# A graph-attention layer in split fp32 on one core: the pairs' projections and values rewritten as pairs of 64-row matmuls

## The reference, cut to what matters

```
h  = relu(layernorm(x))                       # 384 x 1024
q, k, v    = h @ wq.T + bq, h @ wk.T + bk, h @ wv.T + bv
q2, k2, v2 = q @ wiq.T + biq, k @ wik.T + bik, v @ wiv.T + biv    # each (16 heads, 384, 64)
mask = -inf, softplus(w[type]) where an edge is (the last one wins), w[3] on the empty diagonal
attn = softmax(q2 @ k2.T / 8 + mask)          # per head, 384 x 384
y = x + (attn @ v2) @ wo.T + bo
```

## Time and profile before

| | us |
|---|---|
| median of 3 runs | 294.5 |
| span of the profiled execution | 292.6 |
| TensorE busy (1809 matmuls) | 286.9 |
| VectorE busy | 176.3 |
| ScalarE busy | 153.7 |
| GpSimd busy | 149.9 |

### The profile page before, as it was taken

The page is one execution under the profiler, slowest core; times in us unless marked ns, Lnnn a source line. Parts: engine busy times, 40 slices in busy tenths (PEclk is TensorE's granted clock), DMA queues, the critical chain, the costliest instruction groups (busy, mean ns, idle before and its releaser), DMA issues.

```text
span 292.6 us, 4992 instructions
## 1 busy us (share of the span) xinstructions
PE 286.9 (98%) x1809; PEld 266.0 (91%) x1809; DVE 176.3 (60%) x473; ACT 153.7 (53%) x289; POOL 149.9 (51%) x156
## 2 busy tenths in 40 slices
PE   6999999999999999999999999999999999999996
PEld 3799998888899999999999999999999997888885
DVE  4999878696534543454377676665748475835241
ACT  2986343242542344234434685969687879774100
POOL 6452454453454544644400796748393939873000
PEclk9999999999999999999999999999999999999999
DMA  7969965839643344324454043040403122400032
GB/s 269 324 237 266 330 219 165 249 113 341 222 143 106 112 144 146 116 100 146 164 212 146 0 147 119 26 147 0 146 23 124 50 97 72 146 0 0 2 143 72
DMA packets 15818, 40.84 MB, mean 140 GB/s; under 512 B 3481, under 2 KB 4914, under 8 KB 15794
## 3 DMA queue, kind: packets, MB, share of 16 engines
q1 hardware_dynamic: 13346, 38.53, 39.6%
q0 software_dynamic: 2016, 1.21, 1.5%
q10 hardware_dynamic: 432, 0.79, 0.7%
HBM read 37.71 MB, written 2.81 MB: 138 GB/s over the span
## 4 chain that ended last, share of the span: by engine, by line
PE 96%; DMA 1%; DVE 1%; ACT 0%; POOL 0%; issue 0%
PE banks L884 27%; PE banks L885 26%; PE banks L886 26%; PE banks L1015 5%; PE banks L1058 3%; PE banks L1059 3%; PE banks L1030 3%; PE banks L1043 1%; DMA x_sb<-in_x 1%; PE banks L935 1%; DVE stats L711 1%; PE banks L975 1%; PE banks L965 0%; PE banks L978 0%; ACT x_sb L504 0%; POOL rstd L384 0%
## 5 line engine op out<-in xcount | busy, mean ns | idle before, releaser
L426 POOL DMA_INDIRECT cells<-value,cell x51 | 54.5, 1069 | 60.2 <-DMA cells<-value,cell 47.5
L479 ACT ACTIVATE w_hi<-raw 128x1024 fp32r<-128x1024 f32 x50 | 52.6, 1053 | 19.5 <-PE banks L886 17.3
L886 PE MATMUL banks<-a_lo,w_hi 128*128 128x384 f32 x184 | 61.5, 334 | 0.0
L884 PE MATMUL banks<-a_hi,w_hi 128*128 128x384 f32 x184 | 61.5, 334 | 0.0
L885 PE MATMUL banks<-a_hi,w_lo 128*128 128x384 f32 x184 | 61.5, 334 | 0.0
L747 DVE TENSOR_TENSOR w_lo<-raw,w_hi 128x1024 fp32r<-128x1024 f32 x36 | 44.2, 1229 | 12.4 <-ACT w_hi L479 12.2
L452 POOL TENSOR_SCALAR prob<-prob,row_inv 128x384 f32<-128x384 f32 x36 | 22.6, 645 | 42.6 <-DVE row_inv L814 42.6
L884 PEld LDWEIGHTS banks<-a_hi,w_hi 128*128 128x128 f32 x184 | 34.5, 188 | 0.0
L885 PEld LDWEIGHTS banks<-a_hi,w_lo 128*128 128x128 f32 x184 | 34.5, 188 | 0.0
L886 PEld LDWEIGHTS banks<-a_lo,w_hi 128*128 128x128 f32 x184 | 34.5, 188 | 0.0
L399 POOL TENSOR_TENSOR w_lo<-raw,w_hi 128x1024 fp32r<-128x1024 f32 x14 | 33.7, 2410 | 0.0
(11 more groups left out here) (151 smaller groups left out, 611.0 us busy)
## 6 DMA issues: line engine op xcount, KB each, us to landing
raw<-in_slabs SPq DMA_DIRECT2D x56, 512.0 KB, 3.4
work<-key_rows SPq DMA_DIRECT2D x6, 256.0 KB, 5.6
prob<-key_rows SPq DMA_DIRECT2D x6, 256.0 KB, 3.9
x_sb<-in_x SPq DMA_DIRECT2D x3, 512.0 KB, 5.2
out_y<-x_sb SPq DMA_DIRECT2D x5, 256.0 KB, 2.1
cells<-prob SPq DMA_DIRECT2D x2, 576.0 KB, 7.6
cells<-value,cell POOLq DMA_INDIRECT x51, 3.7
x_sb<-in_x ACTq DMA_DIRECT2D x3, 256.0 KB, 4.4
```

The lines of the kernel that those rows point to most:

```text
L426: nc.gpsimd.indirect_dma_start(out=cells[c][:, :], out_offset=bass.IndirectOffsetOnAxis(ap=cell[:, t:t + 1], axis=0), in_=value[:, t:t + 1 ...
L479: nc.scalar.activation(split_place(s)[0], raw[:, s % RAW, :], ACT.Copy).then_inc(slab_hi, 1)
L884: nc.tensor.matmul(psum, w[0], a[0], start=first, stop=False)
L886: return nc.tensor.matmul(psum, w[0], a[1], start=False, stop=last)
```

## The change

It keeps the matrices, the split and the load of the slabs' bytes, and changes how the pairs are worked:

- The q and k projections come out of tiles that hold 64 rows of q above the same 64 rows of k: slabs 16 to 31 alternate between wq and wk and are written interleaved, in twos, into the ring. The second projections are 64-row matmuls, q2 on rows 0 to 63 beside k2 on rows 64 to 127, each into its own bank (`pair_steps`; 48 row pairs for a pair of heads). Slabs 32 to 47 hold one half of the rows of wiq above one of wik.
- `v2` is laid out by 64-row blocks, and so read out in 24 + 24 instructions of 64 x 256 in place of 6 + 6 of 128 x 512.
- The values of both heads run beside each other (`pair_values`, 12 row pairs), with 64 nodes a block; the turns of all eight pairs are 64 by 64, in three runs of 12 (`turn`), the second and the third one behind the other from step 1 on.
- The turned probabilities are read out in three instructions of 768 elements a pair on ACT and on DVE in place of six of 384; reciprocals go in threes.
- q2, k2 and the pair's projection banks (4 and 5) have one buffer; scores and turns share banks 0 to 3, the values have 6 and 7.
- `y_part` moves between the `max_part` of step 0. The output pieces have other banks and another order.
- Early scratch tiles share memory with `prob`, and the bias rows of q and k are copied once (`bias_parts`).

The diff, cut to its core:

```diff
-LO_ALL = QK0 + TILES_AHEAD + 3
+LO_ALL = QK0 + 2 + AHEAD
+SLABS_OF_STEP = [((37 + 2 * j,), (38 + 2 * j,)) for j in range(PAIRS - 1)] + [((51, 52), (53,)), ((54, 55), ())]
...
+        def pair_place(pair):
+            return 6 if pair == 1 else 4
...
+        def last_of(s):
+            return s + 1 - s % 2 if Q0 <= s < QK0 else s
+
         def wait_split_place(eng, s):
...
-                eng.wait_ge(slab_used, s - RING + 1)
+                eng.wait_ge(slab_used, last_of(s) - RING + 1)
...
+            def v2_hi_part(g):
+                for t in range(NT):
...
+                    for half in range(2):
+                        for x in range(2):
+                            own, _ = rows_of(x)
+                            nc.scalar.activation(v2[own, 2 * t + half, pairs_of(g), x, :], v2_from(g, t, half, x),
+                                                 ACT.Copy).then_inc(v2_hi, 1)
...
@@ block.scalar
             for j in range(PAIRS + 1):
+                first, second = SLABS_OF_STEP[j]
+                if 2 <= j < PAIRS:
+                    pair_hi_part(j - 2)
+                for s in first:
+                    split_hi(s)
                 if j < PAIRS:
+                    for n in range(NT):
+                        exp_part(j, n)
                 if j >= 1:
+                    for m in range(2):
+                        pt_hi_part(j - 1, m)
+                if j == PAIRS:
+                    pair_hi_part(PAIRS - 2)
+                if j >= 1:
+                    pt_hi_part(j - 1, 2)
+                if j < PAIRS - 1:
+                    for second_of in range(2):
+                        tile_hi_part(3 * KT + 2 * (j + 1) + second_of)
+                for s in second:
+                    split_hi(s)
+                if j >= 1:
+                    half_part(j - 1)
...
@@ block.vector
             for j in range(PAIRS + 1):
                 if j < PAIRS:
+                    max_part(j, 0)
+                    if j == 0:
+                        y_part(0)
+                    max_part(j, 1)
+                    inv_part(j, 0)
+                    if j == 0:
+                        y_part(1)
+                    max_part(j, 2)
+                    inv_part(j, 1)
+                    if j == 0:
+                        y_part(2)
+                    inv_part(j, 2)
                 if j >= 1:
+                    for m in range(2):
+                        pt_lo_part(j - 1, m)
                 if j == PAIRS:
                     pair_lo_part(PAIRS - 2)
+                if j >= 1:
+                    pt_lo_part(j - 1, 2)
+                if j < PAIRS - 1:
+                    for second_of in range(2):
+                        tile_lo_part(3 * KT + 2 * (j + 1) + second_of)
+                if j >= 1:
+                    head_part(j - 1)
...
+            def pair_steps(pair, first, end):
+                if first == 0:
+                    pe.wait_ge(v2_lo, 4 * GS * NT)
+                    if pair >= 1:
+                        pe.wait_ge(tile_lo, 3 * KT + (0, 0, 2, 6)[pair] if pair < 4 else 3 * KT + 2 * pair)
+                for step in range(first, end):
+                    half, k, p = step // STEPS, step % STEPS // 3, step % 3
...
+                    for x in range(2):
+                        own, _ = rows_of(x)
+                        mm = nc.tensor.matmul(bank[pair_place(pair) + x][:, 0:N], w[own, k * P:(k + 1) * P],
+                                              a[own, block_at % KT, :], start=(step == 0), stop=(step == 2 * STEPS - 1))
...
             def scores(j, n):
+                if n == 0:
+                    pe.wait_ge(tile_lo, 3 * KT + 2 * (j + 1))
+                if n == 2:
+                    pe.wait_ge(masked, chunk_at(j, 0, 1) + 1)
...
+            def turn(pair, m):
+                at, j = turn_place(m), pair + 1
...
+                if m == 2:
+                    pe.wait_ge(pt_lo_ok, turn_at(pair, 0) + 1)
...
+            def pair_values(pair):
...
+                order = [(b, p) for b in range(4) for p in range(2)] + [(b, p) for p in range(2) for b in (4, 5)]
+                for i, (b, p) in enumerate(order):
+                    pe.wait_ge((pt_hi_ok, pt_lo_ok)[p], turn_at(pair, b // 2) + 1)
...
+            pair_steps(0, 0, 2 * STEPS)
+            pair_steps(1, 0, FIRST_STEPS)
+            scores(0, 0)
+            pair_steps(1, FIRST_STEPS, 30)
+            scores(0, 1)
+            pair_steps(1, 30, 40)
+            scores(0, 2)
+            pair_steps(1, 40, 48)
+            pair_steps(2, 0, 8)
+            for j in range(1, PAIRS - 1):
+                scores(j, 0)
+                pair_steps(j + 1, 8, 16)
+                scores(j, 1)
+                pair_steps(j + 1, 16, 24)
+                scores(j, 2)
+                pair_steps(j + 1, 24, 32)
+                turn(j - 1, 0)
+                pair_steps(j + 1, 32, 44)
+                turn(j - 1, 1)
+                turn(j - 1, 2)
+                pair_steps(j + 1, 44, 48)
+                pair_values(j - 1)
+                if j < PAIRS - 2:
+                    pair_steps(j + 2, 0, 8)
+            last = PAIRS - 1
+            scores(last, 0)
+            scores(last, 1)
+            pe.wait_ge(tile_lo, 5 * KT)
+            out_part(0, range(0, 3))
+            scores(last, 2)
+            turn(last - 1, 0)
+            out_part(1, range(0, 3))
+            turn(last - 1, 1)
+            turn(last - 1, 2)
+            out_part(0, range(3, 5))
+            pair_values(last - 1)
+            turn(last, 0)
+            turn(last, 1)
+            out_part(1, range(3, 5))
+            for n in range(2):
+                out_part(n, range(5, 6))
+            turn(last, 2)
+            for n in range(2):
+                out_part(n, range(6, 7))
+            pair_values(last)
+            out_part(2, range(0, 7))
+            out_part(3, range(0, 7))
...
```

More of the change, by code:

```diff
@@ L217, in as_turned, with score_place @@
             return a[:, k, :] if k < KT - 1 else a[:, k, :].rearrange("p (t m) -> p t m", m=P)
[L219 to L236, removed]
+        def score_place(n):
+            return (0, 2, 0)[n]
@@ L627, in _, with pt_hi_part, half_part @@
-            half_part(H - 1)
+            def pt_hi_part(pair, m):
+                both = pair * ROW_BLOCKS + 2 * m + 2
+                act.wait_ge(pt_done, both)
+                act.wait_ge(pt_done_high, both)
+                if pair >= 1:
+                    act.wait_ge(head_done, pair)
+                nc.scalar.activation(as_turned_probs(pt_hi, m), turned(m), ACT.Copy).then_inc(pt_hi_ok, 1)
+            def half_part(pair):
+                act.wait_ge(head_done, pair + 1)
+                b = BIV + pair
+                for x in range(2):
+                    own, other = rows_of(x)
+                    nc.scalar.activation(half_sum[own, :], head_bank[x][other, 0:N], ACT.Identity,
+                                         bias=bias[own, b:b + 1]).then_inc(half_ok, 1)
@@ new lines, in pt_lo_part, with head_part @@
+            def pt_lo_part(pair, m):
+                dve.wait_ge(pt_hi_ok, turn_at(pair, m) + 1)
+                nc.vector.tensor_tensor(as_turned_probs(pt_lo, m), turned(m),
+                                        as_turned_probs(pt_hi, m).bitcast(F32), ALU.subtract).then_inc(pt_lo_ok, 1)
+            def head_part(pair):
+                for x in range(2):
+                    own, _ = rows_of(x)
+                    dve.wait_ge(half_ok, 2 * pair + x + 1)
+                    if x == 0 and pair >= 1:
+                        dve.wait_ge(head_lo, pair)
+                    nc.vector.tensor_tensor(head_out[own, :], head_bank[x][own, 0:N], half_sum[own, :],
+                                            ALU.add).then_inc(head_sum, 1)
@@ new lines, in pair_values @@
+            def pair_values(pair):
+                if pair >= 1:
+                    pe.wait_ge(head_sum, 2 * pair)
+                else:
+                    pe.wait_ge(tile_lo, 3 * KT + 4)
+                order = [(b, p) for b in range(4) for p in range(2)] + [(b, p) for p in range(2) for b in (4, 5)]
+                for i, (b, p) in enumerate(order):
+                    pe.wait_ge((pt_hi_ok, pt_lo_ok)[p], turn_at(pair, b // 2) + 1)
+                    for x in range(2):
+                        own, _ = rows_of(x)
+                        w = v2[own, b, pair, :, :].rearrange("p c d -> p (c d)")
+                        mm = nc.tensor.matmul(head_bank[x][:, 0:N], w, (pt_hi, pt_lo)[p][own, b, :],
+                                              start=(i == 0), stop=(i == len(order) - 1))
```

506 lines of the change are left out of this document (199 added, 307 removed).

## The result

The changed kernel takes 377.39 us (median of six runs, 374.31 to 378.20); the kernel before, run beside it, 294.44. The ratio is 1.279, with the 95% interval 1.274 to 1.284. The forecast was 299.7 us in a range of 294.0 to 303.5: slower, as forecast, but by 27.9% where 1.8% was forecast, and most of it by a cause that the forecast doesn't have. The profiled execution has a span of 372.6 us.

What follows compares the result with a forecast made beforehand. TensorE was taken as the bound. Own work -4.9, the step's chain +5.4, step 0 +1.1 and the end +3.8 us gave +5.4, taken as +5.2: from 294.5 to 299.7 us, range 294.0 to 303.5.

Steps and rivals of the forecast that it cites:

- What I cost at nothing: Items given no time: small `v2` reads, paired slabs, strided operands, POOL's order, SP's loads; lost `v2` cover up to 0.5 us.
- more waits than I see: Rival: further waits, as slabs split too late at the end or first q tiles held by `v2`; 303 to 308 us, chance 0.07.
- The first q tiles: Before the pairs: the second twelve small `v2` reads lie under the first two q and k tiles, enough by 0.1; no cost.
- TensorE's own work: Matmul work: 16 fewer switches between full and half rows, -3.2 us, and cheaper turns, -1.7 us; together -4.9 us.
- the rival of a lost pace: Rival: half rows lose pace in long stretches as weight loads come into the open; about 340 us, chance 0.03.
- The step's chain: Steps 1 to 6: next projections wait for `tile_lo` behind the `pt_lo` reads, 0.9 us six times; +5.4 us.
- the slope: Read-out times for 768 elements extended from 384 and 512: ACT 0.81 us, DVE 0.96 us.
- Step 0: Before pair 1's scores: `y_part` between `max_part` makes DVE's work 8.9 us against TensorE's 7.8; +1.1 us.
- The end: From step 7 on: TensorE waits behind splits, `pt_lo` and `head_lo`, 1.8, 1.2 and 0.8 us; +3.8 us.
- the signs of being wrong: Projections following values without a gap, wide reads under 0.6 us, or ACT's end splits not ahead of its `pt_hi`.
- The first rival: Wide reads cost less than the slope, hiding the step's chain; 293.2 us, or 290 to 291 with the end hidden; chance 0.14.

Runs made afterwards that it cites:

- e1: The changed kernel with slabs 32 to 47 laid out by the host so that each loads as one whole block; 305.74 us, ratio 1.040.
- e7: e1 with the second run of turns at matmul step 36 instead of 44 and the third at 42; 302.38 us, ratio 1.027.
- e9: e5 with pair 6's subtraction done by GpSimd between its splits instead of by VectorE; 293.36 us, ratio 0.9946.
- e10: e1 with the y additions moved from VectorE's step 0 to the query and key stage, and four more matmul steps in step 0; 305.76 us.
- e5: e1 with the edits of e7, e8 and e10, and the first query tile read out ahead of v2's second half; 296.63 us.
- e8: e1 with late splits behind read-outs and norms, pair 6's copy and subtraction behind pair 7's first read-out, its third turns behind the next output piece; 302.69 us.
- e4: e1 with the second run of turns moved from matmul step 44 to 36 and the third to 46; 307.01 us, ratio 1.045.

## Why the prediction was wrong, step by step

**The step that failed** is the last sentence of "What I cost at nothing": "SP issues the same loads; the half slabs have the same bytes." The number of loads and of bytes is the same, and each took some 10.1 us on two engines where whole slabs landed in 3.4 to 3.5 us before. It cost 71.7 of the 77.7 us between forecast and result. The sum costed a transfer by its bytes and never looked at its shape; nor did a rival, "more waits than I see" included. That the result is slower, as forecast, is to that extent luck.

The other 6.0 us are e1 (305.7) against the forecast; they too end above the range. The rival "more waits than I see" (303 to 308 us, 0.07) has this time and one of its causes, the first q tiles held by `v2`. By the terms of the sum, in e1's trace (its rows of the pairs' start and of the first scores stand first):

```profile
146.42 0.44 PE L1062 MATMUL banks<-b_hi,w_hi 64*128 64x384 f32 x2
146.70 0.34 PE L1062 MATMUL banks<-b_hi,w_lo 64*128 64x384 f32 x2
...
158.31 0.35 PE L1081 MATMUL banks<-k_hi,q_hi 64*128 64x384 f32 x2
```

- **The first q tiles: cost at nothing ("enough by 0.1"), +2.05 us** (the pairs start at 146.42 against 144.37). The small reads take 0.40 (ACT) and 0.45 us (VectorE) back to back, forecast 0.28 and 0.33: twelve are 4.8 and 5.4 us, not 3.4 and 4.0. VectorE came to tile 8 at 87.24, and TensorE waited for it until 88.01, with its last matmul started at 86.06.
- **TensorE's own work: -4.9, too large by about 2.** The pace of half rows held: the 67 places from 146.70 to 158.31 are 0.173 us each, weight loads included. So the rival of a lost pace did not come. By the rule of the Trainium skill beside it ("TensorE: Matmul & The Clock Gate", Part 3, The mechanism) each place would have paid for its load; the trace disagrees, now over 67 places. A step without its wait is 13.41 us (e7) against 13.85, a gain of 0.44 where 0.8 was due. The turns cost more apart: in e9 each run of twelve puts 0.43 us between its neighbours (197.49 to 198.09, less one place), 1.28 for three where I had 1.12, and 0.11 remains where projections follow values; the last 0.1 of a step is not explained.
- **The step's chain: +0.9 a step, right.** The wide reads took 792 ns (ACT, median) and 956 ns (VectorE); the slope gave 0.81 and 0.96. In e1 a step loses 0.63 us ahead of the projections and 0.25 within the values (191.93 to 192.53), 0.88. With the smaller gain in own work a step is 14.19 us where the forecast has 13.95 (13.85 less 0.8, plus 0.9): +1.4 over six.
- **Step 0: +1.1, right** (a gap of 1.21 less a place of 0.17 is 1.0), and for the right cause: e10 takes the gap down by 0.7, and gains 0.8 at equal clock.
- **The end: 1.8, 1.2 and 0.8 us.** The three gaps are 1.95, 1.70 and 2.18 us start to start. Without a wait the same neighbours stand 0.03, 0.33 (257.45 to 257.78) and 0.15 apart, so the waits are 1.9, 1.4 and 2.0: +1.5 in sum. The third is the one that was mis-sized, since I took VectorE's subtraction at 0.5 us and it took 1.77 beside a split of GpSimd.
- **Not in the sum: the clock.** After the first of these gaps it fell in e1 for 3.4 us (262 to 265 at 0.50), which costs some 1.4 us. I had gaps at the end and no sentence on what they do to a clock that was full in every slice.

2.05 + 1.4 + 1.5 + 1.4 = 6.35, which is 0.3 more than the 6.0 to be explained; the working does not resolve that. As to the signs of being wrong: with whole slabs, the change as written is 4.0% slower and the forecast of +1.8% had its direction for the reason given. The first rival (293.2 us, or 290 to 291 with the end hidden too) is what e9 comes near, but by an order of work that hides the chain, not by cheaper reads. What is still missing there to the -4.9: about 2 in own work over six steps, the pairs' start 0.45 us later (144.82 against 144.37; 0.25 of it two short gaps at 90 us, behind the small reads), and gaps of 0.3 in step 0 and about 1 at the end.

What stays open: what decides whether the clock falls at the end. In e5 and in e8 it stayed full in some runs (three of nine, two of four) and fell in others, though the program has the same third gap (2.3 us in the profiled execution); a longest gap between 1 and 2 us was not tried. And the excess of 0.05 us in each run of turns that stand apart is measured and not explained.

## What to carry to other kernels

Cost a moved or reshaped transfer by the engines it will run on, not by its bytes alone: if the outermost dimension of its source is 2, look for a share of 2/16 at a constant rate, and issue it as several transfers or lay out the source anew. When a change fuses small operations into wide ones, write out each chain anew, and give every link the earliest place where its input exists: moving one of two turn runs gained almost nothing (e4, 0.4 us at equal clock), both 3.4 us (e7, 4.0). A VectorE subtraction with both operands in SBUF belongs where GpSimd is at rest, or onto GpSimd. Compare small gains at equal mean clock: by the medians e10 gained nothing, at equal clock 0.8 us.

## What the runs showed of the hardware

- A 2x64-row load of 512 KB took some 10.1 us (estimated from its packets) on 2.05 of 16 DMA engines; two loads of 64 rows of the same data cost the kernel no more than one of 128 (305.82 against 305.74 us).
- VectorE's 128x384 subtraction with both operands in SBUF took 558 ns alone and 1767 and 2735 ns (e1, e5) beside GpSimd's 128x1024 split, and ended 0.4 us behind it. The wide `pt_lo` with one operand in PSUM kept 0.96 us beside splits in e9. The Trainium skill ("SBUF — State Buffer", "SBUF: two separate sides") states that the port pair that VectorE and GpSimd share is an exclusive lock: whichever of a VectorE operation with two SBUF inputs and a GpSimd operation that reads SBUF starts first has it for the whole instruction, and the other is blocked. The trace agrees in that the subtraction starts behind the split and ends 0.4 us after it. The same subtraction took 834 ns in the kernel before, also beside a split, and was no term of my sum.
- Two 64-row matmuls side by side keep the pace of one full one, 0.173 us, for 67 places on end (e1).
- With the gap of 2.3 us in e5, full clock turned into half for 6.8 us in the profiled execution, and the mean clock was 0.988 to 0.994 in six of nine runs and 0.999 to 1.000 in three. With 0.5 us in its place (e9) it was 0.998 to 1.000 in all twelve.
